# A two-layer transformer kernel whose work order is planned with other weights, hand-over times and landing margins

## The reference

```python
for layer in (0, 1):
    sa, ca, ga, sb, cb, gb = modulation(silu(c) @ wmod)       # per sequence
    h = layernorm(x) * (1 + ca) + sa
    q, k, v = project(h)                                      # 16 heads of 8 features
    att = softmax(scale * q @ k.T)                            # causal in layer 1
    x = x + ga * (att @ v @ w_out + b_out)
    h = layernorm(x) * (1 + cb) + sb
    w, idx = top_k(softmax(h @ gate), 2)                      # two of 8 experts a token
    if layer == 0:
        y = sum(w[e] * (silu(h @ w1[e]) * (h @ w3[e])) @ w2[e] for e in idx)
        y = y + (silu(h @ sw1) * (h @ sw3)) @ sw2
    else:
        y = sum(w[e] * square(relu(h @ W1[e])) @ W2[e] for e in idx)
    x = x + gb * y
```

## Time and profile before

| | us |
|---|---|
| median of three runs | 1072.07 |
| lowest and highest run | 1069.85, 1079.47 |
| profiled execution: span | 1051.9 |
| PE busy in it | 979.1 |
| VectorE busy | 821.8 |
| ScalarE busy | 746.4 |
| GpSimd busy | 456.9 |

### The profile page before, as it was taken

One profiled execution on the slowest core, in us unless ns is written; L12 is line 12 of the kernel. 1 busy time (PEld: TensorE's weight loads), 2 busy tenths in 40 slices (PEclk: granted clock), 3 DMA queues, 4 the chain that ended last, 5 costly groups with the idle time before them and its releaser, 6 DMA issues.

```text
span 1051.9 us, 28537 instructions
## 1 busy us (share of the span) xinstructions
PE 979.1 (93%) x11295; PEld 521.8 (50%) x11295; DVE 821.8 (78%) x1657; ACT 746.4 (71%) x1241; POOL 456.9 (43%) x546
## 2 busy tenths in 40 slices
PE   7688887889999999999999999999999989999998
PEld 6211222222655555445656666667665544455566
DVE  6978999976999788678977689777877667577556
ACT  4458775779664777886676775677757897776865
POOL 5220131243215415642443654455544665855564
PEclk9879999999999999999999999999999999999999
DMA  6932444254754685694666787878787767411100
GB/s 178 248 90 67 126 111 119 68 171 138 227 182 122 201 245 162 180 272 140 197 198 199 217 244 243 249 211 260 213 269 223 212 183 190 101 62 65 36 11 21
DMA packets 120500, 174.79 MB, mean 166 GB/s; under 512 B 19912, under 2 KB 84296, under 8 KB 120368
## 3 DMA queue, kind: packets, MB, share of 16 engines
q1 hardware_dynamic: 114112, 159.87, 51.4%
q0 software_dynamic: 5680, 12.33, 4.0%
q10 hardware_dynamic: 576, 0.79, 0.3%
HBM read 114.21 MB, written 58.59 MB: 164 GB/s over the span
## 4 chain that ended last, share of the span: by engine, by line
PE 55%; DVE 20%; DMA 9%; ACT 6%; issue 5%; POOL 3%; SPq 0%; POOLq 0%; DVEq 0%; ACTq 0%
PE ps L771 17%; PE ps L897 12%; DVE nm L1110 10%; PE ps L773 9%; PE ps L880 6%; PE ps L857 6%; DMA gr<-d_y,pos 5%; ACT ES L1445 4%; DMA d_h<-hx,pos 2%; DMA d_h<-r,pos 1%; POOL gr L1679 1%; PE ps L799 1%; ACT xn L1370 1%; PE ps L885 1%; PE ps L862 1%
## 5 line engine op out<-in xcount | busy, mean ns | idle before, releaser
L1110 DVE TENSOR_REDUCE nm<-ps 128x2 f32<-128x1024 f32 (+3 forms) x512 | 503.8, 1017 | 97.5 <-PE ps L862 52.5
L1445 ACT ACTIVATE ES<-ps 128x1024 f32<-128x1024 f32 (+1 forms) x448 | 416.8, 963 | 85.5 <-PE ps L880 52.9
L897 PE MATMUL ps<-ES,VS 128*9 128x512 f32 (+3 forms) x2048 | 221.8, 518 | 2.1 <-DVE hdx L1294 0.9
L857 PE MATMUL ps<-KS,QS 48*128 48x512 bf16 (+3 forms) x1110 | 180.6, 357 | 23.3 <-DVE nm L1110 16.1
L880 PE MATMUL ps<-QS,KS 51*128 51x512 bf16 (+3 forms) x1072 | 172.4, 348 | 17.2 <-DVE nm L1110 8.1
L880 PEld LDWEIGHTS ps<-QS,KS 51*128 51x128 bf16 x1072 | 50.6, 94 | 147.3 <-ACT ES L1445 56.1
L857 PEld LDWEIGHTS ps<-KS,QS 48*128 48x128 bf16 x1110 | 51.4, 95 | 139.1 <-DVE nm L1110 60.6
L1679 POOL DMA_INDIRECT gr<-d_y,pos x80 | 83.5, 1043 | 79.9 <-DMA gr<-d_y,pos 52.8
L771 PE MATMUL ps<-hsT,wst 128*128 128x128 f32 x676 | 95.4, 284 | 1.1 <-DVE rj L1235 0.5
L771 PEld LDWEIGHTS ps<-hsT,wst 128*128 128x128 f32 x676 | 82.2, 191 | 19.9 <-issue 17.0
L1605 POOL TENSOR_TENSOR sp<-sr,sp 128x512 bf16<-128x512 f32 x32 | 37.2, 1175 | 89.7 <-ACT sp L1406 89.6
(11 more groups left out here) (233 smaller groups left out, 1539.9 us busy)
## 6 DMA issues: line engine op xcount, KB each, us to landing
wst<-we SPq DMA_DIRECT2D x92, 576.0 KB
d_u<-US SPq DMA_DIRECT2D x60, 256.0 KB
KS<-d_k SPq DMA_DIRECT2D x62, 192.0 KB, 4.2
QS<-d_q SPq DMA_DIRECT2D x62, 192.0 KB, 4.9
hs<-d_h SPq DMA_DIRECT2D x25, 256.0 KB, 3.4
d_y<-ys SPq DMA_DIRECT2D x25, 256.0 KB
d_q<-sp SPq DMA_DIRECT2D x16, 384.0 KB
d_k<-sp SPq DMA_DIRECT2D x16, 384.0 KB
```

The costliest lines, as they stand in the source:

```text
L857: mm = eng.matmul(psum[:, bank[u][a], c:c + n], QS[m][r:r + KA, pr, 128 * t1:128 * t1 + 128], KS[m][r:r + KA, pr, 0:n], start=True, stop=i ...
L897: mm = eng.matmul(psum[32 * a:32 * a + 9, b, q0:S], VS[i % 3][:, j1, 4 * g + a, :], ES[(2 * EXP[i, g, j] + a // 2) % NES][:, a % 2, c:c + ...
L1110: ins = eng.tensor_reduce(nm[f][:, :].rearrange("p (a c) -> p a c", a=2)[:, :, 4 * pr + t1], ps2("score", i, f, pr, t)[:, :, c:c + n], AX. ...
L1445: eng.activation(ES[(2 * n + pp) % NES][:, :, 0:w], ps2("bscore", i, f, g, j, pp)[:, :, 0:w], ACT.Exp, scale=SC1 if i >= NB else SC0).then ...
```

## The change

It touches the planner alone. `plan()`, its units and dependencies, and all code that issues instructions stay as they are (its lines stand 22 further down, so that line 857 is 879 and so on).

- Weights: `SERVICE` replaces the weights of 21 kinds of unit, among them the gather and scatter (1.35 to 1.1) and the scaling of gathered tiles (0.38 to 0.58).
- Hand-overs: a unit's lag to its followers was 0.43 + 0.05 on PE, 0.26 + 0.05 on VectorE, 0.28 + 0.05 on ScalarE, 0.2 on GpSimd. It is now 0.39 on PE and 0.22 on the three others.
- Landings: a DMA's lag had 0.6 added; now 0.5, and 2.0 for scatters and gathers.
- Mode prices: `SWITCHES` has other values.
- Urgencies: the tables have other numbers, a table row for each family instead of shared ones, and none of the layer offsets for m, c, x, rr, r.

```diff
@@ -70,29 +70,53 @@
 
 
 
-SHIFT = {"bscore": -0.04, "c": -16.7, "d": 26.54, "early": -28.49, "expo": -16.03, "f": -27.19, "g": -35.51, "ld": -17.69, "m": 36.89, "max": -9.4, "p": -4.5, "pv": 0.21, "r": 12.19, "rowmax": 4.69, "rr": -32.16, "s": 0.79, "score": -0.08, "stack": 22.3, "t": -2.16, "u": 36.55, "v": -32.48, "w": 0.47, "x": 1.09}
...
+SHIFT = {
+    "bscore": -0.04, "c": -209.911, "d": -10.55, "early": -9.237, "expo": 24.426, "f": -82.771, "g": -21.724, "ld": -73.255, "m": 3.318, "max":
...
+LATE = {
+    "expo": 5.179, "f": -25.56, "g": 21.984, "max": -82.701, "p": 1.13, "pv": 0.004, "rowmax": 28.019, "score": 0.018, "stack": 7.054, "t":
...
 NUDGE = {
-    "p": [-36.05, 22.22, -1.54, -36.98, -4.51, 2.71, -41.46, -17.43, -24.71, 2.32, 9.36, 13.64, -18.7, -12.76, 16.01, 36.68],
-    "score": [-9.52, -2.53, 0.06, -0.08, 0.1, -0.0, -0.01, 0.01, 0.06, -0.05, -0.15, -0.1, -0.1, 0.04, 10.55, 10.46],
...
+    "bscore": [0.032, 0.021, -0.021, -99.561, 0.008, -0.036, -0.228, -0.13, -1.693, -0.192, -27.744, -38.544, 0.0, -39.458, -11.676, 18.288],
+    "c": [-2.309, -0.32, -1.641, -4.947],
...
-TIED = {"early": "p", "v": "t", "stack": "p", "rowmax": "score", "bscore": "expo", "rr": "r"}
+WHOLE = "m", "c", "x", "rr", "r"
+
+
+SERVICE = {"g_w": 0.58, "rr_pos": 2.3, "max_sub": 0.19, "max_hi": 0.13, "max_mid": 0.18, "f_lg": 0.33, "f_gt": 0.17, "p_norm": 1.53, "f_norm": 1.53, "rr_oh": 0.35, "m_fin": 1.4, "t_w": 2.24, "p_rstd": 1.88, "f_rstd": 1.88, "p_lo": 1.12, "g_x": 4.1, "d_add": 1.28, "d_x": 2.92, "r_sc": 1.1, "g_ga": 1.1, "d_rg": 2.4}
+
+
+READY = 0.22
 
 
 
 class Plan:
@@ -104,26 +128,24 @@
              "x_w": 2.0, "c_h": 3.2, "ld": 1.0, "r_sc": 0.27, "g_ga": 0.27, "d_out": 1.0, "max_st": 0.25, "max_ld": 0.5,
              "t_st": 0.15, "g_gc": 0.4, "m_st": 0.1}
 
-    LAG = {"PE": 0.43, "DVE": 0.26, "ACT": 0.28, "POOL": 0.2, "SP": 1.8}
+    HANDOFF = {"PE": 0.17 + READY, "DVE": READY, "ACT": READY, "POOL": READY, "SP": 0.0}
 
     def __init__(self):
         self.work = {}
 
-    def add(self, engine, key, weight, urgency, after=(), lag=None, mode="full", opens=0, closes=()):
-        lag = self.LAG[engine] if lag is None else lag
-        if lag >= 1.0 or key[0] in self.MOVES:
-            lag += LATER
-        elif engine in ("PE", "DVE", "ACT"):
-            lag += SPARE
-        family, i = key[0].split("_")[0], key[1] if len(key) > 1 else None
+    def add(self, engine, key, weight, urgency, after=(), lag=0.0, mode="full", opens=0, closes=()):
+        moves = engine == "SP" or key[0] in ("r_sc", "g_ga", "d_out", "m_ld")
+        lag = lag + (INDIRECT if key[0] in ("r_sc", "g_ga") else LANDING) if moves else self.HANDOFF[engine]
+        family, i = key[0].split("_")[0], key[1] if len(key) > 1 and isinstance(key[1], int) else None
         urgency += SHIFT.get(family, 0.0)
-        if i in range(NB, N):
-            urgency += LATE.get(family, 0.0)
-        if i in range(N - 3, N):
-            urgency += LAST.get(family, 0.0)
-        table = NUDGE.get(TIED.get(family, family))
-        urgency = round(urgency, 3) + (table[i] if table and isinstance(i, int) else 0.0)
-        self.work[key] = (engine, weight, round(urgency, 3), after, lag, mode, opens, closes)
+        if i is not None:
+            if family not in WHOLE:
+                if i >= NB:
+                    urgency += LATE.get(family, 0.0)
+                if i >= N - 3:
+                    urgency += LAST.get(family, 0.0)
+            urgency += NUDGE[family][i] if family in NUDGE else 0.0
+        self.work[key] = (engine, SERVICE.get(key[0], weight), urgency, after, lag, mode, opens, closes)
 
     @staticmethod
     def choose(banks, n, t):
@@ -138,18 +160,18 @@
         self.work = {k: (*v[:3], [a for a in v[3] if a in self.work], *v[4:]) for k, v in self.work.items()}
         nxt = {k: [] for k in self.work}
         left, ready = {}, {}
-        cands = {e: [] for e in self.LAG}
+        cands = {e: [] for e in self.HANDOFF}
...
 WARM = 12, 3, 3
-LATER, SPARE = 0.6, 0.05
+LANDING, INDIRECT = 0.5, 2.0
 WEARLY = 0.2
 SLACK, SWITCH = 0.05, 0.1
-SWITCHES = {("full", "half"): 0.1, ("full", "cols"): 0.1, ("half", "full"): 0.08, ("half", "cols"): 0.08,
-            ("cols", "full"): 0.11, ("cols", "half"): 0.113,
-            ("half", "any"): 0.08, ("any", "half"): 0.105,
-            ("full", "any"): 0.0, ("cols", "any"): 0.0, ("any", "full"): 0.0, ("any", "cols"): 0.0}
+SWITCHES = {("full", "half"): 0.11, ("full", "cols"): 0.15, ("full", "any"): 0.02,
+            ("half", "full"): 0.15, ("half", "cols"): 0.14, ("half", "any"): 0.17,
+            ("cols", "full"): 0.11, ("cols", "half"): 0.08, ("cols", "any"): 0.02,
+            ("any", "full"): 0.0, ("any", "half"): 0.1, ("any", "cols"): 0.15}
 
 XAT, XLEN = (2.6, 1.6), (2.0, 1.6)
 SPREAD = 2.5, 2
```

More of the change, by code:

```diff
@@ L69, in wait_ge @@
             self.seen[sem.name] = value
-SHIFT = {"bscore": -0.04, "c": -16.7, "d": 26.54, "early": -28.49, "expo": -16.03, "f": -27.19, "g": -35.51, "ld": -17.69, "m": 36.89, "max": -9.4, "p": -4.5, "pv": 0.21, "r": 12.19, "rowmax": 4.69, "rr": -32.16, "s": 0.79, "score": -0.08, "stack": 22.3, "t": -2.16, "u": 36.55, "v": -32.48, "w": 0.47, "x": 1.09}
-LATE = {"bscore": 0.01, "c": 19.16, "d": -2.55, "early": -13.05, "expo": 23.45, "f": -2.64, "g": 7.82, "ld": 18.63, "m": -11.22, "max": -30.65, "p": -16.16, "r": 27.31, "rowmax": 7.18, "rr": -14.21, "s": 25.03, "score": 0.02, "stack": -53.64, "t": -3.93, "u": -28.23, "v": 10.39, "w": -54.04, "x": 5.06}
@@ L95 @@
-TIED = {"early": "p", "v": "t", "stack": "p", "rowmax": "score", "bscore": "expo", "rr": "r"}
+SHIFT = {
[3 rows of a table added]
+}
+LATE = {
+    "expo": 5.179, "f": -25.56, "g": 21.984, "max": -82.701, "p": 1.13, "pv": 0.004, "rowmax": 28.019, "score": 0.018, "stack": 7.054, "t":
+    7.779, "u": -48.957,
+}
+LAST = {
+    "bscore": -32.383, "d": 1.816, "expo": -1.556, "f": 22.972, "max": -49.189, "p": -28.632, "pv": 3.356, "score": 6.988, "stack": -5.034, "t":
+    6.626, "u": 43.712,
+}
+NUDGE = {
+    "bscore": [0.032, 0.021, -0.021, -99.561, 0.008, -0.036, -0.228, -0.13, -1.693, -0.192, -27.744, -38.544, 0.0, -39.458, -11.676, 18.288],
+    "c": [-2.309, -0.32, -1.641, -4.947],
+    "d": [0.0, 0.0, 0.0, 0.0, 0.0, 0.0, 0.0, 0.0, -3.806, 0.301, 52.84, 42.433, 44.148, 0.628, 9.374, -17.3],
+    "early": [-36.554],
+    "expo": [-2.654, 0.0, 47.595, -0.715, 13.501, -22.385, -0.567, -107.436, 78.139, -15.048, -177.843, 129.756, -4.918, 22.599, 25.617, 8.27],
+    "f": [202.847, 21.602, -14.888, 21.184, 58.671, -31.004, -0.318, -10.994, 0.0, -11.816, -88.806, -189.114, 0.0, 41.224, 7.958, 0.0],
+    "g": [-46.366, 8.309, -4.184, 65.142, 5.377, 57.974, -0.487, -101.733, -15.815, -11.594],
+    "m": [-17.804, 20.369],
+    "max": [0.0, -10.112, 5.438, -2.949, -68.776, -0.421, -24.949, -10.807, 1.448, -62.693, 20.76, -31.715, 31.684, 153.035, 0.0, -23.282],
[3 rows of a table added]
+    "rowmax": [-14.776, 8.117, 37.451, -40.151, 11.688, 134.881, -11.165, 24.172, 13.114, 23.32, -0.671, -74.38, 5.904, 18.999, -1.292, 58.12],
+    "rr": [-1.652, 6.595, 0.0, 11.317, 20.794],
+    "s": [6.488, -23.169, 0.207, -14.723, -34.033, -45.718, -0.558, -64.604],
+    "score": [0.163, 0.175, 0.06, -0.08, 0.106, 0.0, -0.015, 0.011, 0.065, -0.05, -0.15, -62.279, -31.126, 79.33, -8.025, 4.324],
+    "stack": [-39.109, 10.794, 0.0, -6.373, -14.125, 13.371, 17.625, 18.589, -25.555, 1.476, 14.141, -9.433, -2.549, 52.192, 0.816, -95.784],
+    "t": [123.815, -74.872, -21.379, -16.301, 19.19, 1.165, 15.092, -12.944, 117.748, 1.105, -9.117, 70.841, 40.909, -10.571, 2.294, 5.822],
+    "u": [-3.83, 7.184, -0.205, 0.0, -3.875, 1.888, 14.859, -16.141, 4.916, 5.996, -15.398, 24.453, -62.921, 14.509, 5.305, 15.755],
+    "v": [-76.288, -45.108, 18.183, -79.099],
+    "x": [-0.02, 0.01, 0.002, -0.093, -10.848],
+}
@@ L147, in settle @@
                 cands[e].append(k)
-        free = {e: 0.0 for e in self.LAG}
+        free = {e: 0.0 for e in self.HANDOFF}
         banks = {b: 0.0 for b in range(8)}
@@ L151, in settle @@
         held, mode, moved = {}, None, 0.0
-        todo = {e: [] for e in self.LAG}
+        todo = {e: [] for e in self.HANDOFF}
         bank, emptied = {}, {}
```

3 lines of the change are left out of this document (removed), and 14 rows, old and new, of tables (NUDGE, SHIFT).

## The result

| | before, us | changed, us | ratio (95% interval) |
|---|---|---|---|
| first measurement, 12 runs each | 1075.09 | 1070.02 | 0.9954 (0.9933 to 0.9975) |
| second (again_after) | 1075.85 | 1071.17 | 0.9936 (0.9905 to 0.9967) |
| third (after_here) | 1079.04 | 1074.07 | 0.9926 (0.9894 to 0.9958) |
| fourth (after_last) | 1056.17 | 1053.37 | 0.9964 (0.9933 to 0.9995) |

A forecast was written before the change was run, and what follows sets the result against it. TensorE (PE), busy 979.1 of 1051.9 us, was taken as the bound, behind 250 us. Terms 7 - 6 - 6 - 8 + 1 = -12 us gave a span of 1039.9, plus 20.2: 1060 us, 1.1% faster, range 1037 to 1085.

The forecast's parts named there:

- nothing comes of it: Rival, whole kernel: gains from ring and gathers about equal what the strips cost, time within 1% of 1072; chance 0.31.
- Part 1, +7: PE's expert and dense stages: 200 products issued whole instead of as strips cost 0.035 us each, 7 us slower.
- Part 2, 800 to 900 us, -6: Between 800 and 900 us: wider gather margins end ScalarE's 5.4 us of waits, PE gets about that back, 6 us faster.
- asked for 95: Sign between 800 and 900 us: PE busy 95 of 100 us there.
- Part 2, the middle, -6: Long middle up to 800 us: wider gather and scatter margins recover a little over a third of PE's 16.4 us idle.
- Part 3, -8: Attention ring, 50 to 250 us: shorter planned hand-overs and measured weights recover 8 of PE's 27.3 us idle.
- slower, by the short hand-overs: Rival, PE's queue in the attention ring: hand-overs planned too tight make PE wait, 1093 us; chance 0.24.
- Part 4, +1: Start: the load of the first negated maxima is issued 1 to 3 us later, mostly hidden, 1 us slower; end 0.
- The clock: I expect nothing from it: Whole kernel: clock at its upper level (2.4 GHz) nearly throughout, so no gain or loss from it.
- The addition of 20.2 us: Whole kernel: the runs' median, 1072.07, lies 20.2 us above the profiled span, so 20.2 is added to the forecast span.

The follow-up runs named there:

- again_after: The changed kernel, word for word, timed again on a slower chip: 1071.17 us against 1075.85 for the kernel before, ratio 0.9936.
- after_here: The changed kernel, word for word, timed again on a slower chip: 1074.07 us against 1079.04 for the kernel before, ratio 0.9926.
- after_last: The changed kernel, word for word, on a quick chip: 1053.37 us against 1056.17 for the kernel before, ratio 0.9964; traced span 1052.1 us.
- after_nostrips: The changed kernel, order kept, every open product issued whole instead of in strips: 1060.94 us, 1.0054 of the kernel before.
- before_here: The kernel before, word for word, profiled on a quick chip: one run, 1057.62 us, span 1055.7 us.
- after_oldmargins: The changed kernel planned with the old landing margin (0.6 us for every DMA), all else new: 1133.54 us, 1.0725 of the kernel before.

## Why the prediction was wrong, by its steps

The sum was -12 us and the measured change is -2.8 to -5.1. The forecast lay at 1.1% and the measured gain at 0.4 to 0.7%; "nothing comes of it" was the rival that came nearest.

**Part 1, +7, about right, for an incomplete reason.** L793 has 2202 records in all for L771's 1802 (902 for 676 in its largest group). PE's busy time shows nothing here: the 1.7 us more of the pair are less than what traces of one kernel differ by. By the order without strips the price is 14.7 us for 461 products, 0.032 each, or 6.4 us for the 200. By the timeline, where 0.1 us of a mode change is separate, it is 0.015 to 0.025 a product, 3 to 5 us, and the number of changes (858, 857) adds nothing. In the new order the 261 products that stay strips are worth 7.6 us (1060.94 of after_nostrips against 1053.37 of after_last, with before at 1055.92 and 1056.17), 0.029 each. The two kernels without strips, in one measurement, give 4 to 6 us for the 200. The term stands, with 4 to 6 in place of 7.

**Part 2, 800 to 900 us, -6: -3.9 on the quick chip.** ScalarE's waits for gathers, 5.4 us in the first trace and 3.7 in before_here, are gone from after_last's list of that window, and PE is busy 96.87 of 100 where I asked for 95. On the slower chips PE stands at 91.23 and below, so there I would have called it failed. GpSimd's own wait for gathers did not fall (10.5 and 11.7 us in the pair).

**Part 2, the middle, -6: this is the step that failed.** PE's idle time there was to fall by 6 us and rose by 5.3. I took "a little over a third" of 16.4 us idle for the margins' doing, with no wait that names a gather behind it: PE's waits between 300 and 800 us, then and in before_here, name VectorE and ScalarE, and of the DMAs only a load of scattered rows with 0.2 and 0.5 us. What the runs showed instead is where the time went. 3.2 of the 5.3 us lie between 250 and 300, where PE idles 4.6 us for 1.4: a lead of ten us at the 128th exponential became a lag of six at the first expert. By the traces the last two scatters of the group stand behind a step that waits 6.72 us for VectorE, and the load of their rows goes out 5.3 us later. That is order around the very scatters to which the margin belongs. Behind 300 us PE's idle time did not fall either (18.5 and 20.6), while waits moved from ScalarE's scalings to GpSimd's additions. That the wide margin caused the order at the scatters is possible and not shown, since after_oldmargins moved everything at once.

**Part 3, -8: -6.5, about right.** PE's waits in the ring, in after_last, against 8.0 and 6.7 us in before_here and the earlier trace rows:

```profile
PE ps L879 <- DVE nm L1132: 6.9, 17, 0.8
...
PE ps L902 <- DVE nm L1132: 2.1, 7, 0.5
```

The exponent products' waits for maxima fell from 6.7 us to 2.1, and the scores' nearly stayed. Whether the short hand-overs did it, or the weights and urgencies that came with them, was not separated. Of the rival "slower, by the short hand-overs" nothing was seen.

**Part 4, +1: right.** In the first trace of the changed kernel the load of maxima is issued 2.8 us later and the first exponential is where it was (the earlier trace rows have 54.75 and 62.93).

```profile
57.54 0.57 SPq L1819 DMA_DIRECT2D QS<-d_m  x2
```

```profile
62.82 1.02 ACT L1467 ACTIVATE ES<-ps 128x1024 f32<-128x1024 f32 x1
```

**"The clock: I expect nothing from it"** failed in its place and not in its sum. On the slower chip of again_after the mean clock over all runs was 0.977 for both kernels. But the doubled products are keyed to attention products of the old order; in the new one stretches from 90 and from 264 us run at the lower level, where before_here has 1.00, and doubling others gave 3.7 to 6.1 us. That this came by the clock is read from the windows above and not tested apart. The sum had nothing for this, and it is the second part of the miss.

**The addition of 20.2 us** was a comparison across chips. It cost nothing in the ratio, since both sides carried it.

## What to carry to other kernels

Book a gain from idle time only against a wait that names the cause; a share of unnamed idle time in a long stretch is a wish. When a planned wait moves off one engine, look where it turns up again, and when a lead in one kind of work is gone a little later, follow the chain of the next kind (here scatter, landing, load, transpose) in both traces to the first step that has lost it. After any reordering, look again at what was fitted to the old order by hand, here the doubled products for the clock.

## What the runs showed of the hardware

- A change from column work to whole work on TensorE costs 0.12 us at one place and 0.1 in the mean of some 60; an f32 product of 128x128 takes 0.015 to 0.025 us less as four column strips than whole, at two places.
- One program differs by 1.8 to 2.3% between chips (medians of 1055 to 1056 and of 1075 to 1079 us), with the mean clock of its runs at 0.980 to 0.981 and at 0.976 to 0.977.
- Across the 29 runs of the kernel before in one measurement, 0.01 of mean clock goes with 7 us of time, with much scatter; across another's 23 with 10 us.
- Two matmul records of 128x512 f32 took 1.02 us at the upper clock level and 2.08 at the lower, which began behind 2.16 us of idle.
- A pair of scatters issued at the same time in two traces (254.74 and 254.76 us for the last) landed 2.2 us behind the last issue in one and 5.9 in the other.
